# Attention values by row tiles, in two parts a quad, and matrix-engine loops whose heads are placed and whose way back is announced

## The reference

```python
qkv = x @ Wqkv                               # 16 heads of 64
q = l2norm(q) * qs;  k = l2norm(k) * ksc     # then rotary tables on both
sim = einsum('bhwie,bhwje->bhwij', bq, bk2) * QK_SCALE   # windows of 32 queries, 64 keys
attn = softmax(where(mask, -max, sim), -1)
out = einsum('bhwij,bhwje->bhwie', attn, bv2)            # the "values"
x = out @ Wo + x
...                                          # layer norm, gated feed-forward, + x
```

## Time and profile before

| | before |
|---|---|
| median of 3 runs | 3267.62 us (3261.32 to 3268.75) |
| the profiled execution | 3268.94 us, span 3267.1 us |
| mean granted clock of TensorE | 0.976 of full |
| PE busy | 2997.5 us, 92% of the span |
| PE weight loads busy (beside the matmuls) | 1884.2 us, 58% |
| DVE busy | 2863.2 us, 88% |
| ACT busy | 2279.6 us, 70% |
| POOL busy | 1791.3 us, 55% |

### The profile page before, as it was taken

One profiled execution on the slowest core, in us unless ns is written; L12 is line 12 of the kernel. 1 busy time (PEld: TensorE's weight loads), 2 busy tenths in 40 slices (PEclk: granted clock), 3 DMA queues, 4 the chain that ended last, 5 costly groups with the idle time before them and its releaser, 6 DMA issues.

```text
span 3267.1 us, 93385 instructions
## 1 busy us (share of the span) xinstructions
PE 2997.5 (92%) x37658; PEld 1884.2 (58%) x37896; DVE 2863.2 (88%) x2671; ACT 2279.6 (70%) x3707; POOL 1791.3 (55%) x823
## 2 busy tenths in 40 slices
PE   8689998999899998999999999999999999999997
PEld 4355555555555555555566655665665665665563
DVE  5688888888888888888999989999999999999995
ACT  4467676667667676667666777777777777777774
POOL 8555554555555555555454556655655655555551
PEclk9899999999999999999999999999999999999998
DMA  9544544544444454455344445445445445445442
GB/s 318 167 110 100 141 113 101 136 107 110 112 126 107 105 141 106 104 135 137 87 120 106 103 102 146 114 109 146 113 110 146 112 109 148 111 109 149 112 116 65
DMA packets 254585, 400.99 MB, mean 123 GB/s; under 512 B 51148, under 2 KB 84872, under 8 KB 254280
## 3 DMA queue, kind: packets, MB, share of 16 engines
q1 hardware_dynamic: 254280, 396.41, 46.5%
HBM read 64.64 MB, written 19.92 MB: 26 GB/s over the span
## 4 chain that ended last, share of the span: by engine, by line
PE 40%; DVE 24%; ACT 19%; issue 12%; POOL 1%; SPq 1%; DVEq 0%; DMA 0%; ACTq 0%; POOLq 0%
PE ps L842 6%; PE ps L860 5%; PE ps L800 5%; PE ps L876 5%; PE ps L821 4%; PE ps L781 4%; ACT f_ab L1088 4%; DVE f_mx L1356 4%; DVE f_p L1359 3%; ACT f_u L1087 3%; PE ps L782 3%; PE ps L783 3%; DVE f_p L1371 3%; ACT ps L1099 3%; ACT f_p L1105 3%
## 5 line engine op out<-in xcount | busy, mean ns | idle before, releaser
L1285 POOL TENSOR_TENSOR f_w<-f_w,f_ab 128x1024 f32<-128x1024 f32 x192 | 549.1, 2860 | 527.1 <-DVE f_w L1336 527.1
L1290 POOL TENSOR_TENSOR f_ab<-f_w,f_rn 128x1024 f32<-128x1024 f32 x192 | 595.4, 3101 | 418.5 <-DVE f_rn L1346 410.0
L1281 POOL TENSOR_TENSOR f_u<-f_u 128x512 f32<-128x512 f32 x384 | 570.4, 1498 | 458.7 <-ACT f_u L1087 445.7
L1087 ACT ACTIVATE f_u<-ps 128x512 f32<-128x512 f32 x768 | 466.7, 608 | 183.6 <-PE ps L783 148.5
L1336 DVE TENSOR_TENSOR f_w<-f_ab,f_tan 128x1024 f32<-128x1024 f32 x384 | 494.4, 1328 | 71.4 <-ACT f_ab L1088 69.1
L1088 ACT ACTIVATE f_ab<-ps,f_pa 128x512 f32<-128x512 f32 x768 | 541.2, 705 | 1.2
L781 PE MATMUL ps<-f_xh,f_wh 128*128 128x512 f32 x768 | 395.1, 514 | 149.5 <-issue 82.3
L842 PEld LDWEIGHTS ps<-f_tb,f_v 128*64 128x64 f32 x6144 | 395.8, 137 | 109.9 <-issue 75.7
L842 PE MATMUL ps<-f_tb,f_v 128*64 128x160 f32 (+1 forms) x6144 | 441.9, 297 | 17.1 <-DMA f_tb<-f_pt 13.5
L1099 ACT ACTIVATE ps<-ps 128x512 f32<-128x512 f32 x384 | 204.7, 574 | 346.8 <-PE ps L800 346.4
L860 PE MATMUL ps<-f_ot,f_wout 128*128 128x512 f32 x768 | 367.2, 601 | 10.0 <-issue 6.7
(11 more groups left out here) (164 smaller groups left out, 4760.7 us busy)
## 6 DMA issues: line engine op xcount, KB each, us to landing
f_kb<-f_ab SPq DMA_DIRECT2D x384, 256.0 KB, 3.6
f_qb<-f_ab SPq DMA_DIRECT2D x384, 256.0 KB, 3.6
f_tb<-f_pt SPq DMA_DIRECT2D x1344, 64.0 KB
f_wh<-split_w SPq DMA_DIRECT2D x48, 384.0 KB, 4.4
f_wl<-split_w SPq DMA_DIRECT2D x48, 384.0 KB, 4.2
a_w_raw<-wqkv SPq DMA_DIRECT2D x24, 384.0 KB, 4.7
split_w<-a_w_hi SPq DMA_DIRECT2D x24, 384.0 KB, 4.6
split_w<-a_w_lo SPq DMA_DIRECT2D x24, 384.0 KB, 5.6
```

The source lines that it names most:

```text
L1087: nc.scalar.activation(u[:, i, :], bank("qk", g, i), ACT.Square).then_inc(sq_done.sem, 1)
L1281: nc.gpsimd.tensor_tensor(u[:, 2 * i + 1, :], u[:, 2 * i, :], u[:, 2 * i + 1, :], ALU.add).then_inc(sq_sum[i].sem, 1)
L1285: nc.gpsimd.tensor_tensor(w[:, 0:2, :], w[:, 0:2, :], ab[:, k % 2, 0:2, :], ALU.add).then_inc(q_sum.sem, 1)
L1290: nc.gpsimd.tensor_tensor(ab[:, k % 2, 0:2, :], w[:, 0:2, :], rn[:, 0:1, :].broadcast_to([128, 2, N]), ALU.mult).then_inc(rope_q.sem, 1)
```

## The change

It has three parts.

**Values.** A quad is computed in two parts. Every matmul takes half of a token tile, 64 key rows, on a 64 by 64 tile of the array, and streams three windows (96 columns, 64 at the sequence's end) instead of five. The four tiles of the array take two heads and two row halves at once: in part 0 the upper rows serve the first pair of heads into bank 3 while the lower rows serve the second pair into bank 4, in part 1 they are exchanged, which is what `half = pair ^ part` does. A part is 16 matmuls, and ahead of them stands one null matmul of eight zero columns over the whole array, which starts (part 0) or ends (part 1) the accumulation. Part 1 waits for part 0 by a semaphore of its own, `o_part`, and other work is placed between the two where the order allows. Both `o_ready` signals come at the end of part 1. `values(-1, 0)` moves ahead of `project_out(2)`.

**tb.** It holds three windows a tile instead of five. SP issues the same number of DMAs with the same bytes into other places, and waits for both `o_ready` signals.

**Loops.** PE's two loops get `hint_back_edge`, which puts a prefetch hint for the backward branch at the loop's first instruction, and `head_slot` 0, which places the loop's head at the first instruction of a block of 256.

```diff
+                def loop(eng, first, end):
+                    if eng.engine != mybir.EngineType.PE:
+                        return eng.Fori(first, end)
+                    return nc.Fori(first, end, engines=bass.OrderedEngineSet([eng.engine]), hint_back_edge=True, head_slot={eng.engine: 0})
...
-                    with eng.Fori(1, RET1) as s:
+                    with loop(eng, 1, RET1) as s:
...
-                    with eng.Fori(RET2 + B, STEPS - B + 1) as s:
+                    with loop(eng, RET2 + B, STEPS - B + 1) as s:
...
-                            sp.wait_ge(o_ready[1].sem, now.count(o_ready[1], g - 1))
+                            for i in range(2):
+                                sp.wait_ge(o_ready[i].sem, now.count(o_ready[i], g - 1))
...
-                        def values(g):
+                        def values(g, part):
+                            if part == 1:
+                                pe.wait_ge(o_part.sem, now.count(o_part, g))
+                                value_products(g, part)
+                                return
...
-                            for pair in range(2):
-                                for tile in range(TILES):
-                                    windows = 5 if tile < TILES - 1 else 4
-                                    for h in (2 * pair, 2 * pair + 1):
-                                        rows = slice(64 * (h % 2), 64 * (h % 2) + 64)
-                                        last = nc.tensor.matmul(ps[rows, NO[pair], 128 * tile:128 * tile + WIN * windows],
-                                                                v[:, tile, d0:d0 + 64], tb[:, 0:windows, 8 * (h % 2) + 2 * tile + h // 2, :],
...
+                            nc.tensor.matmul(ps[:, NO[0], 0:8], identb[:, :], nothing, start=part == 0, stop=part == 1, skip_group_check=True)
+                            for tile in range(TILES):
+                                for h in range(2):
+                                    for pair in range(2):
+                                        half = pair ^ part
+                                        at = 128 * tile + 64 * half
+                                        windows = 3 if at < N - 64 else 2
+                                        rows, d0 = slice(64 * half, 64 * half + 64), 256 * (g % QUADS) + 128 * pair + 64 * h
+                                        last = nc.tensor.matmul(ps[64 * h:64 * h + 64, NO[pair], at:at + WIN * windows],
+                                                                v[rows, tile, d0:d0 + 64], tb[rows, 0:windows, 8 * h + 2 * tile + pair, :],
...
-                            project(0, range(4))
+                            project(0, range(3))
+                        if prev:
+                            values(-3, 0)
+                        if cur:
+                            project(0, (3,))
...
-                            values(-3)
+                            values(-3, 1)
                             project_out(0)
...
-                            values(-2)
-                        if cur:
-                            project_v(0, range(2, TILES))
+                            values(-2, 0)
+                        if cur:
+                            project_v(0, (2,))
+                        if prev:
+                            values(-2, 1)
+                        if cur:
+                            project_v(0, (3,))
...
                         if prev:
+                            values(-1, 0)
                             project_out(2)
-                            values(-1)
+                            values(-1, 1)
...
-                            project_v(1, range(2, TILES))
-                            values(0)
+                            project_v(1, (2,))
+                            values(0, 0)
+                            project_v(1, (3,))
+                            values(0, 1)
```

More of the change, by code:

```diff
@@ L471, in build_hybrid @@
         o_read = [per_quad(f"o_read{i}", ahead=3) for i in range(2)]
+        o_part = per_quad("o_part", 2)
         wo_ready, fs_done = Signal("wo_ready"), Signal("fs_done", 2)
@@ L489, in build_hybrid @@
         PE_USES = [(1, -1), (1, 0), (1, 2), (2, -2), (3, -5), (3, -4), (3, -3), (3, 0), *((4, c) for c in range(-4, 1)),
-                    *((8, c) for c in (-12, -8, -7, -6, -5, -4, -3, -2, -1, 0)), *((16, c) for c in range(-15, 1)),
+                    *((8, c) for c in (-12, -10, -8, -7, -6, -5, -4, -3, -2, -1, 0)), *((16, c) for c in range(-15, 1)),
                     *((128, c) for c in range(-64, 33, 32)), *((512, c) for c in range(-640, -255, 128))]
@@ new lines, in value_products @@
+                        def value_products(g, part):
+                            nothing = mask[:, 288:768:64]
+                            nc.tensor.matmul(ps[:, NO[0], 0:8], identb[:, :], nothing, start=part == 0, stop=part == 1, skip_group_check=True)
[8 more added lines that the diff above has]
+                                                                v[rows, tile, d0:d0 + 64], tb[rows, 0:windows, 8 * h + 2 * tile + pair, :],
+                                                                start=part == 0 and tile == 0, stop=part == 1 and tile == TILES - 1, skip_group_check=True,
+                                                                tile_position=(64 * half, 64 * h))
+                                        if part == 1 and tile == TILES - 1 and h == 1:
+                                            last.then_inc(o_ready[pair].sem, 1)
+                                        if part == 0 and tile == TILES - 1 and h == 1:
+                                            last.then_inc(o_part.sem, 1)
```

21 lines of the change are left out of this document (11 added, 10 removed).

## The result

The changed kernel takes 3213.94 us (median of 4 runs, 3209.46 to 3220.69) against 3267.68 us of the kernel before in the same comparison. The ratio is 0.9841, with a 95% interval of 0.9818 to 0.9864: faster by 53.7 us, 1.6%. The forecast was 134 us, and 3214 lies above its range of 3095 to 3205.

The account below looks back on a forecast made before the run. PE and DVE were both taken as near their limits, with PE's time counting up to `scores(0)`. Loop 1 116.6, loop 2 11.9 and other steps 5.5 gave 134.0 us off 3268.9: 3134.9 us, range 3095 to 3205.

Parts of the forecast that it names:

- 0.7 us a step for the values: `values(-3)` and `values(-2)`, ahead of `scores(0)`, each save 0.38 us in parts; 0.76 cut to 0.7 us a step.
- `values(-1)`: Part 0 ahead of `project_out(2)` waits 1 us for DMAs, `project_out(3)` 0.5 for copies; priced at nothing, uncovered up to 0.5.
- The way back: Loop 1 on PE would run as loop 2 did, without the stall for instructions: 5.13 us a step over 20 steps.
- 0.9 us of moved work: At `values(-1)`: with about 0.8 us of cover, it was to hold the 1.5 us of waits.
- The slower rival: Longer body no longer stays resident, both loops stall at the way back: 3322 us, chance of slower 0.06.
- The values' range for a round: Each of a part's 8 rounds of matmuls on PE takes 84 to 114 ns.
- The way back gains, the values don't: Rival: a round takes 114 ns or worse, so only loop 1's gain comes: 3166 us, chance 0.12.
- DVE waiting at L1385: Sign of being wrong: DVE's residual, which needs `project_out(3)`, has to wait for it; no size given.
- A wait on "issue" ahead of the scores: Sign of being wrong: PE waits above 1 us for instructions at the way back or ahead of the scores.

Follow-up runs that it names:

- The loops' part alone: Kernel before with the placed heads and the way-back hint on PE's two loops, values as they were: 3163.71 us, ratio 0.9661.
- place alone: Kernel before with PE's loop heads at the start of a block, no hint, values as they were: 3167.54 us, ratio 0.967.
- hint alone: Kernel before with the way-back hint on PE's loops, heads where they fall, values as they were: 3170.21 us, ratio 0.9678.
- values-only kernel: Changed kernel with plain loops, neither hint nor placed heads: 3331.95 us, ratio 1.0158 to the kernel before.
- part moved back: Changed kernel with `values(-1, 0)` back behind `project_out(2)` in the steps without retention: 3157.03 us, ratio 0.9638 to the kernel before.
- quad moved whole: Kernel before with the loops' change, values in one piece, `values(-1)` moved ahead of `project_out(2)`: 3200.57 us, ratio 0.9774.
- part 0 half way: Changed kernel with `values(-1, 0)` between the two matmuls of `project_out(2)`: 3170.16 us, ratio 0.97 to the kernel before.
- the two with DVE made lighter: Inverse-sum multiplication cut to 64 of 1024 columns: kernel before with loops' change, 3114.7 us; changed kernel with `values(-1, 0)` behind `project_out(2)`, 3101.53 us.

## Why the prediction was wrong

The sum was 134.0 us; 53.7 were measured. Two of its terms failed: the 0.7 us a step for the values, for which DVE had no wait to give back, and above all `values(-1)`, priced at nothing, which cost 1.2 us a step. By its terms:

- **The way back, 102.6 us forecast: right.** The loops' part alone gives 3275.2 - 3163.7 = 111 us in its series, and loop 1 went from 66.58 to 61.43 us, 5.15 us for the 5.13. **The way there was another.** The head's place was to take the stall at the way back away (the theory that the run with the place alone tests). The runs show instead that loop 1 is no longer streamed: from its first mark to its last, 179 blocks were fetched in before and none in the changed kernel. What counts in them is whether the body stays resident. A block is 256 instructions in the trace: behind loop 2 of before, from 3030 to 3236 us, 20 packets of 16.4 KB came for 5112 recorded instructions of PE. Counting in the compiled program the blocks that a body touches from where its head stands gives the pattern. Loop 2 of before starts at instruction 137 of its block and touches seven; it stayed without help (no block fetched from its first mark to its last), and so did the placed body of 1612 instructions (74 blocks in the whole run, none inside the loops). Loop 1 of before, from instruction 254, touches eight and was streamed (nine blocks a step); with the hint alone, at the same place, it stayed (74 in the whole run). The changed body touches eight even from a block's start: streamed without the hint (nine a step), resident with it (86 in the whole run, none between the marks of either loop). The two loops of the values-only kernel, from about instruction 70, touch eight too and were streamed (nine a step); their heads are far from a block's end, so the two instructions ahead of it are not what made loop 1 stream. Seven blocks stayed by themselves, eight only with the hint, in each case run. What goes with the head's place in a streamed loop is the stall at the way back. From L883's end to the next L781 pass 3.56 to 4.60 us at the 20 returns of loop 1 of before (82.3 us of "issue" in all at L781), whose head stands two instructions ahead of a block's end; where the head is a block's first instruction (changed kernel without the hint) it is 0.58 to 1.20 us over 37 returns, and from instruction 70 at most 0.87. Two packets of instructions stand at a return in either case: before, at that of the earlier trace rows, one starts at 959.72 under the records of L883 and takes 1.30 us, and one at 963.18, in the stall, and takes 1.12; in the changed kernel without the hint one at 486.70 and one at 490.58, around L908's end at 489.45, where no stall is. The second packet is 1.12 of the 3.56 us; which block it brings and what the rest of the time is, no run shows. Without that stall a streamed step was still 1.8 to 3.1 us longer than a resident one, so taking it away would not have been enough.
- **"Ahead of `scores(0)` lie two quads ... 0.7 us a step": wrong.** The part's cost was right (0.93 us for 0.92), but the place where it was to count wasn't there. The 1.19 us in the earlier trace rows are one occurrence in 17 steps. Of the 31.4 us that the sum has for the values, 6.7 came (part moved back against loops alone). Dividing the idle time by its count in the view of waits would have shown it before.
- **"values(-1) ... priced at nothing": wrong, and the largest error.** The wait for the DMA was forecast at 1 us and measured at 1.22, the one for the copies at 0.5 and measured at 0.37. Two things failed. The cover: L860 ended 0.80 us ahead of L1385, 0.86 in the step from the loop's middle, and the prediction took all of that as slack. In the changed kernel `project_out(3)`'s records end at 2126.16 and L1428, which waits for nothing else, starts at 2126.59: 0.43 us pass between the two in any case, so the slack was 0.43. And the "0.9 us of moved work" is no cover: all of the quad's work still stands ahead of `project_out(3)`, and only what the parts save comes off, 2.22 less 2 x 0.93, or 0.36. The waits, for their part, cost more than they show. The matmuls ahead of them start 0.23 us apart and their records take 0.40, so an idle time counted from a record's end is some 0.17 short: PE lost 1.39 and some 0.5 us at the two places, 1.9 in all. Less 0.36 and 0.43 that is 1.1; with 0.10 more, since the records of `project_out(3)` take 1.98 us where they took 1.88, it comes to the 1.15 us a step that DVE waited. As DVE runs back to back behind the residual, it went into the step whole: 1.2 us a step, 44.6 us over the 37 returns by the part moved back, where the bound without cover was put at "up to 0.5". The spans of the two profiled executions differ by 52.0 us; the rest lies ahead of the first mark and behind the last loop.
- **The slower rival: its mechanism was half right.** The longer body is no longer kept without the hint, and then both loops are streamed (3331.95 us measured for 3322 forecast in that rival). It didn't come about since with the hint the changed kernel fetched no block in either loop.
- The values' range for a round, 84 to 114 ns, held: 0.82 us from the null matmul's follower to the next kind, in eight rounds, is 102 ns. "The way back gains, the values don't", 3166 us, had a chance of 0.12. Its number is that of the loops-only kernel (3163.7), but its reason, a round of 114 ns or worse, did not come about: the values gained little because DVE didn't wait for PE.
- The sign of being wrong that the prediction named last, "DVE waiting at L1385", is the one that showed in the loops (as L1428). A wait on "issue" ahead of the scores stands only in unrolled steps, 1.93 us at most, where before has up to 1.27. In before the weight loads of the scores, PEld's rows, have two such waits above 1 us, 1.43 and 1.33, and 2.4 and 2.6 us ahead of their ends a packet of instructions starts (1695.52 and 1841.54); in loop 2, which fetches none, the longest is 0.64.

The 7.4 us lost behind the last loop can be placed in part. From the last mark of loop 2 to the end the profiled executions took 241.5 us in before, 242.5 with the loops' part alone, 249.3 with the quad moved whole, 249.0 in the changed kernel and 245.4 with the part moved back. PE's waits on "issue" of more than 0.6 us in that stretch go the same way: 2.9, 2.9, 8.5, 7.4 and 5.4 us in all. In the changed kernel two of them stand ahead of the moved part, one of them here:

```profile
3118.80 0.17 PE L854 MATMUL ps<-f_mask,f_identb 128*128 128x8 bf16 x1 [1.53 <-issue]
```

So the move costs in those steps too; each figure is from one execution.

What stays open: what those waits on "issue" are for, why L1350 is shorter with the values in parts, and why eight blocks stay resident only with the hint.

## What to carry to other kernels

Divide a wait by its count before building on it, and take it from a step in the loop's middle: an idle time seen once may belong to the loop's first pass. A piece of work moved ahead of another pays at its new place for whatever it waits for there, and everything behind it on its engine pays too; if the engine that waits for it runs back to back, the only cover is the slack of a steady step, here 0.43 us. And a hardware loop's body should be counted in blocks of instructions from where its head stands: in this kernel a body that touched eight and was streamed cost 5.1 us a step in loop 1 of before against one of seven, and the longer body without the hint 1.8 to 3.1 us against the same with it.

## What the hardware showed that was not expected

A streamed loop costs at two places. In loop 1 of before PE stalled 3.56 us at the way back. In the changed kernel without the hint there was no such stall, and a step was still 1.8 us (loop 2) to 2.2 us (loop 1) longer than with it. There SP's issues of the DMAs of `tb` took up to 2.04 us where 0.59 is the median, and at most 0.67 in the loops of the changed kernel, which are resident. The same long issues stand in loop 1 of before (up to 2.02 us) and not in its loop 2 (at most 0.67). They come together with the nine blocks a step; that the fetches cause them is only argued, since no run fetched blocks in another way. Fetches are not needed for every long issue either: three resident kernels (part moved back, hint without place, part 0 half way) have a single one each, of 1.36 to 1.70 us, and the two with DVE made lighter have some of 0.9 to 1.1 us.

The null matmul of eight columns with its change of tiling costs little: 0.11 us from its start to the first 64 by 64 tile.
